# Context keys and values of a decoder's second layer, projected ahead of the first layer's experts and kept in DRAM

## The chip, the cores and the metric

The program runs on one core of a Trainium2 chip. The metric is the device time of one execution in microseconds (us), lower is better. PE is the matrix engine (TensorE), DVE the vector engine, ACT the scalar engine, POOL is GpSimd, SP is the engine that here does nothing but issue DMAs. ACT and POOL issue DMAs too, each on a queue of its own.

## What is computed

A two-layer decoder on x (4 sequences of 512 tokens, width 256) and a context of the same shape. Every step adds its result to x after a layer norm:

```python
x = x + L0_attn(layernorm(x))                 # Mamba block, then attention with 4 heads and a gated FFN
x = x + L0_xattn(layernorm(x), ctx, mask)     # 16 heads of 64, squared relu in place of softmax
x = x + L0_ffn(layernorm(x))                  # 8 experts, each token goes to one
x = x + L1_attn(layernorm(x))                 # block-local causal attention, blocks of 64, 16 heads of 16, rope
x = x + L1_xattn(layernorm(x), ctx, ctx)      # full softmax attention over the context
x = x + L1_ffn(layernorm(x))                  # 16 experts that pick 128 tokens each, and a shared FFN
```

What matters here is `L1_xattn`:

```python
q = (Q @ Wq + bq).reshape(B, L, H, E)
k = (K @ Wk + bk).reshape(B, S, H, E)         # K = V = ctx: neither k nor v depends on x
v = (V @ Wv + bv).reshape(B, S, H, E)
scores = jnp.einsum('blhe,bshe->bhls', q, k)
A = jax.nn.softmax(scale * scores, axis=-1)
out = jnp.einsum('bhls,bshd->blhd', A, v).reshape(B, L, H * E)
return out @ We + be
```

## The kernel before

All engines have a hand-written program each, and wait for one another through semaphores. A `Lane` is a ring of PSUM banks: PE fills a tile (`fill` waits until the tile that was in the bank has been drained), another engine takes it (`take`) and counts `drained` up. SBUF is one array, `arena`, that the stages use one after the other at fixed places, so a buffer of a later stage lies where an earlier one's data were.

The stages, in order of time:

1. Layer 0, per batch (four times): the Mamba block, attention, FFN and cross-attention, 0 to about 1512 us. For the last batch PE, DVE and ACT end with a norm and with the router's logits.
2. Routing (from 1512 us). DVE works out, in some 20 small steps, which slot each token gets (`slot_i`) and which expert each tile of 128 slots belongs to (`te_i`). PE gives it two small matmuls (L962, L963) and then has nothing until tokens have been scattered: POOL scatters 16 chunks to `slots_x` with an indirect DMA each (L2517), ACT waits for all of them and loads the first tile `xg0` (L1633), PE transposes it (L967) and DVE copies it out (`take_slots`, L2127). After the routing steps DVE also zeroes and fills the selection matrices `sel_q` and `sel_k` (six memsets, L2118, and 16 copies, L2123), and sets the ones that stand beside each head's values in `v1o` (L2119).
3. The experts of layer 0: 23 tiles of 128 slots, two buffers (`w1b`, `w2b`, 1 MB each) for the weights, loaded by SP. A tile's weights are asked for as soon as the tile two before it has used the same buffer; PE waits at a tile's start for both matrices of it. PE does W1 (L610, 32 matmul records), the transposes of the next tile (L967) and W2 (L990, 16 records). ACT applies the Gelu and issues the loads of the tokens (`xg0`, 128 KB each, L1639). From tile `W1_AT` = 3 on it also issues, one per tile, the 16 loads of layer 1's weights (`w1_loads`, L1641, 16 to 512 KB each, some 5 MB in all). POOL stores each tile's result to `slots_y` (L2522).
4. POOL gathers the results back (L2526), PE turns the first batch's (`turn_y`, L1033), and layer 1's loop over the batches b = 0..3 begins.
5. One turn of that loop. PE: the rope projections, the values `v2`, then the context keys `yk` (L1089, from `ctxB`, 512 KB that SP loads per batch); then the block scores (L1101), which wait for `qk_here`, 16 small SBUF-to-SBUF DMAs that SP issues one after the other; masks, softmax, transposes (L1112) and weighted sums (L1129) of the four pairs p = 0..3 of blocks follow. Between them lie, for b of 1 and more, the four gate tiles of the shared FFN of the batch before (`ffn_gate(f, m)`, f = b - 1): ACT applies the Gelu (L1665), DVE multiplies (L2178). Then the output projection, a norm, the stacks of the keys (L1168, drained by ACT), the queries `yq` and the context values `yv` (both on the lane that DVE drains). DVE splits the queries into three bf16 parts in five steps (`split_step`, L2215 and L2217), adds the bias to the values (L2264), and PE builds the query stacks (L1168, `w(kq_step, 10)`) and goes on to the cross-attention's scores (L1208).
6. The router and the 16 experts of layer 1, from about 2600 us.

## Time and profile before

| | us |
|---|---|
| median of 3 runs (lowest to highest) | 3049.41 (3048.18 to 3050.52) |
| the profiled execution, its own time | 3046.58 |
| its span in the profile | 3044.8 |
| PE busy | 2701.1 (89%) |
| DVE busy | 1507.2 (50%) |
| ACT busy | 1150.0 (38%) |
| POOL busy | 682.0 (22%) |
| mean granted PE clock, share of 2.4 GHz | 0.936 |

The profile gives for each engine what it did and, before each instruction, how long the engine had been idle and what ended that. PE's fp32 matmuls of 512 columns appear as two records each, so one tile of two such products has four. "PEclk" is the clock that PE was granted: 1.00 is 2.4 GHz and 0.50 is 1.2 GHz. A transfer's "landing" is the time from its issue until its data are there.

### The profile page before, as it was taken

How to read it: one execution, taken by the hardware profiler on the slowest of the kernel's cores; microseconds unless marked ns; L12 is line 12 of the kernel's file. 1: busy time of each engine (PE TensorE's matmuls, PEld its weight loads, DVE VectorE, ACT ScalarE, POOL GpSimd, SP SyncE). 2: the span in 40 equal slices, each digit the busy share in tenths (PEclk: the TensorE clock that was granted, in tenths of full speed). 3: DMA queues.
4: the chain of work that ended last, by engine and by line, in shares of the span. 5: the costliest groups of instructions: out<-in, count | busy, mean ns of one | idle time of the engine just before them, and what ended most of it. 6: DMA issues, size and time to landing. Idle time of an engine off the chain costs nothing. (4 is left out here: it accounts for less than half of the span.)

```text
span 3044.8 us, 40557 instructions
## 1 busy us (share of the span) xinstructions
PE 2701.1 (89%) x16440; PEld 1580.9 (52%) x16481; DVE 1507.2 (50%) x2382; ACT 1150.0 (38%) x1989; POOL 682.0 (22%) x364
## 2 busy tenths in 40 slices
PE   7679999999999999999769888988898988699997
PEld 4265535653285426653368753452543533488776
DVE  5565356733784277635611156446544554644332
ACT  4673245533472255424322235345344343011111
POOL 0254044801571065503320200000000000022222
PEclk9889999999999999999889979999999899799998
DMA  4540003100120003000179610100100101044442
GB/s 191 218 156 22 1 0 115 36 1 1 59 92 1 1 1 129 22 1 0 43 272 335 243 20 7 22 22 1 22 21 1 22 7 73 29 148 158 161 157 64
DMA packets 62130, 218.76 MB, mean 72 GB/s; under 512 B 12293, under 2 KB 28122, under 8 KB 45178
## 3 DMA queue, kind: packets, MB, share of 16 engines
q1 hardware_dynamic: 45802, 187.39, 17.0%
q0 software_dynamic: 9568, 18.75, 2.5%
q10 hardware_dynamic: 6576, 10.05, 0.9%
q8 instruction: 130, 2.13, 0.3%
q14 instruction: 54, 0.44, 0.0%
HBM read 171.98 MB, written 39.99 MB: 70 GB/s over the span
## 5 line engine op out<-in xcount | busy, mean ns | idle before, releaser
L610 PE MATMUL psum<-arena 128*128 128x256 f32 (+7 forms) x4160 | 1081.6, 411 | 67.8 <-ACT arena L1488 11.5
L610 PEld LDWEIGHTS psum<-arena 128*128 128x128 f32 (+1 forms) x4160 | 678.7, 199 | 422.8 <-issue 312.4
L2500 POOL TENSOR_TENSOR arena<-arena 128x1024 f32<-128x1024 f32 x128 | 300.0, 2377 | 111.8 <-DVE arena L1958 96.6
L1958 DVE TENSOR_TENSOR_SCAN arena<-arena,psum 128x512 f32<-128x512 f32 x256 | 291.5, 1201 | 26.5 <-PE psum L751 18.2
L751 PEld LDWEIGHTS psum<-arena 128*128 128x128 f32 x2048 | 243.2, 198 | 47.6 <-ACT arena L1518 40.3
L751 PE MATMUL psum<-arena 128*128 128x128 f32 x2048 | 253.9, 284 | 1.9 <-issue 1.9
L2535 POOL DMA_INDIRECT arena<-xn,arena x32 | 31.6, 988 | 959.0 <-DVE arena L2442 907.2
L2507 POOL TENSOR_TENSOR arena<-arena 128x1024 f32<-128x1024 f32 x32 | 76.0, 2374 | 655.0 <-ACT arena L1606 655.0
L2272 DVE TENSOR_REDUCE arena<-psum 128x1 f32<-128x512 f32 x256 | 162.9, 684 | 84.3 <-PE psum L1208 71.2
L2052 DVE SCALAR_TENSOR_TENSOR arena<-psum,arena 128x1024 f32<-128x1024 f32 x128 | 156.8, 1243 | 80.4 <-PE psum L896 80.1
L1606 ACT ACTIVATE arena<-arena 128x1024 f32<-128x1024 f32 x128 | 146.7, 1146 | 110.0 <-DVE arena L2052 109.9
L1750 ACT ACTIVATE arena<-psum 128x1024 f32<-128x1024 f32 x128 | 129.3, 1024 | 115.6 <-PE psum L1230 115.1
L1790 ACT ACTIVATE arena<-psum 128x256 f32<-128x256 f32 x128 | 49.2, 384 | 320.8 <-PE psum L610 320.8
L1511 ACT ACTIVATE arena<-arena 128x512 f32<-128x512 f32 x256 | 163.0, 708 | 0.0
L2511 POOL TENSOR_TENSOR arena<-arena 128x1024 f32<-128x1024 f32 x64 | 151.2, 2362 | 10.2 <-ACT arena L1606 1.3
L907 PE MATMUL psum<-arena 128*64 128x512 f32 x512 | 138.2, 617 | 15.5 <-ACT arena L1606 7.4
L896 PE MATMUL psum<-arena 64*128 64x512 f32 x512 | 142.5, 638 | 2.7 <-ACT arena L1584 2.7
L2036 DVE RECIPROCAL arena<-arena 128x256 f32<-128x256 f32 x64 | 110.9, 1743 | 46.2 <-ACT arena L1598 46.2
L1405 PE MATMUL psum<-arena 128*128 128x256 f32 x512 | 117.5, 382 | 0.0
L1518 ACT ACTIVATE arena<-arena 128x128 f32<-128x128 f32 x256 | 81.6, 390 | 82.6 <-PE psum L751 60.6
L2465 DVE TENSOR_TENSOR arena<-arena,psum 128x256 f32<-128x256 f32 x128 | 53.2, 421 | 115.7 <-ACT arena L1790 115.2
L1723 ACT ACTIVATE arena<-psum 128x512 bf16<-128x512 f32 x128 | 75.9, 596 | 81.1 <-PE psum L1168 78.5
(298 smaller groups left out, 3210.3 us busy)
## 6 DMA issues: line engine op xcount, KB each, us to landing
arena<-in_W SPq DMA_DIRECT2D x46, 1024.0 KB
arena<-c_rows SPq DMA_DIRECT2D x32, 512.0 KB, 3.8
arena<-in_Wg SPq DMA_DIRECT2D x16, 1024.0 KB, 5.0
arena<-in_Wu SPq DMA_DIRECT2D x16, 1024.0 KB, 7.6
arena<-in_Wd SPq DMA_DIRECT2D x16, 1024.0 KB, 10.0
arena<-in_xT SPq DMA_DIRECT2D x8, 512.0 KB, 5.4
zs_all<-arena SPq DMA_DIRECT2D x4, 1024.0 KB, 3.9
ut_all<-arena SPq DMA_DIRECT2D x4, 1024.0 KB, 8.8
```

Source lines behind the costliest of these rows:

```text
L610: r = mm(dst, w, x, start=i == 0, stop=i == len(pairs) - 1)
L751: r = mm(bank[4 + c][:, q * P:(q + 1) * P], duT[:, q, c * P:(c + 1) * P], diag[n % 2][:, q, :], start=True, stop=True)
L896: i = mm(bank[2 + 2 * (u % SBUFS) + r], xkT[64 * r:64 * r + 64, hp, kc * P:(kc + 1) * P], xqT[64 * r:64 * r + 64, hp, :], start=True, stop ...
L907: i = mm(bank[0][64 * r:64 * r + 64, :], v1[:, kc, 2 * hp + r, :], t2[u % TBUFS][:, r, :], start=kc == 0, stop=kc == NC - 1)
L1511: A_(dA[n % 2][:, c, :], dl[:, c, :], ACT.Exp, scale=aneg[:, c, n:n + 1]).then_inc(dA_ready.sem, 1)
L1606: A_(t2[u % TBUFS], rl[u % RBUFS], ACT.Square, scale=0.125, bias=vec[:, V_NB:V_NB + 1])\
L1750: A_(pr1[v % 4], psum[:, 4 + 2 * (v % 2):6 + 2 * (v % 2), :], ACT.Exp).then_inc(p1_ready.sem, 1)
L1958: V.tensor_tensor_scan(hs[n % 3][:, c, :], dA[n % 2][:, c, :], bank[4 + c], 0.0, ALU.mult, ALU.add)\
L2052: V.scalar_tensor_tensor(rl[u % RBUFS], t, minus_nb8, bound[:, kc, :].unsqueeze(1).broadcast_to([P, 2, L]), ALU.max, ALU.min).then_inc(rel ...
L2272: V.reduce_max(negm1[:, qc, h:h + 1], t, AX.X, negate=True).then_inc(s1_max.sem, 1)
L2500: nc.gpsimd.tensor_tensor(h, h, c_all[:, n % CBUFS, :].unsqueeze(1).broadcast_to([P, 2, L]), ALU.mult)\
L2511: nc.gpsimd.tensor_tensor(t, t, t2[kc], ALU.add).then_inc(tsum_step.sem, 1)
```

## The change

- The keys (with bias `bk`) and the values (with bias `bv` and the ones) of all four batches are projected right behind PE's two routing matmuls, for which the four contexts are loaded into the place of `y_all` (the views `xnf`). Lane `LCK` (banks 2 and 3) is drained by ACT into `kf_st`, lane `LCV` (banks 4 to 7) by DVE into `v1o_st`. The order on PE is 4 value tiles, 8 key tiles, 4 value tiles.
- PE waits until both lanes are drained before it goes on to the transposes of the first expert tile. DVE's drains stand behind its routing steps and ahead of its work on `sel_q` and `sel_k`.
- ACT stores `kf_st` (512 KB) and `v1o_st` (1 MB) of batch b to DRAM scratch at expert tile `KV_AT` + b, b = 0..3, with `KV_AT` = 3. `w1_loads` move from ACT, beside the expert tiles, to SP, in the last batch of layer 0 behind the drains of `xq`, with the loads of the four contexts ahead of them.
- In layer 1's loop `yk` and `yv` are gone, with their drains on ACT and DVE (the removed lines of those two engines are not shown), and SP loads `kf` and `v1o` of a batch from the scratch: for batch 0 once the experts' last store has landed, later ones once the buffers are free.
- `ffn_gate(f, 0)`, with its Gelu and its product, moves from behind `block_scores(0)` to ahead of it.

```diff
+        kf_all, v1o_all = dram("kf_all", (B, P, KD * L)), dram("v1o_all", (B, P, NC * LH * 2 * LE))
...
+                if b == B - 1:
+                    sp.wait_ge(LA.drained.sem, LA.drained.at(LA.upto("xq", 8), b))
+                    for i in range(B):
+                        sp.dma_start(xnf[i], batch("ctxT", i)).then_inc(ld_cB.sem, 16)
+                    for dst, src in w1_loads:
+                        sp.dma_start(dst, A[src]).then_inc(ld_w1.sem, 16)
...
-            def load_ctx(b):
-                sp.dma_start(ctxB, A["ctxT"][b:b + 1].rearrange("a p k n -> p (a k) n")).then_inc(ld_cB.sem, 16)
+            def load_kv(b):
+                if b >= 1:
+                    sp.wait_ge(kq_step.sem, kq_step.at(5, b - 1))
+                sp.dma_start(kf.rearrange("p a b -> p (a b)"), kf_all[b]).then_inc(ld_kf.sem, 16)
+                if b >= 1:
+                    sp.wait_ge(LBO.full.sem, LBO.full.at(4, b - 1))
+                sp.dma_start(v1o.rearrange("p c h e -> p (c h e)"), v1o_all[b]).then_inc(ld_v1o.sem, 16)
...
             load_x(0)
+            sp.wait_ge(st_kv.sem, st_kv.at(16 * 2 * B))
             load_x(1)
-            sp.wait_ge(scattered.sem, 16 * CH)
-            load_ctx(0)
+            for j in range(2):
+                sp.wait_ge(st_y[j].sem, st_y[j].at(0, (NT0 + 1 - j) // 2))
+            load_kv(0)
...
+            pe.wait_ge(ld_w1.sem, 16 * len(w1_loads))
+            pe.wait_ge(ld_cB.sem, 16 * B)
+            def value_tile(n):
+                t = LCV.fill(pe, 0, "v", n)
+                for c in range(2):
+                    o = (2 * (n % 2) + c) * P
+                    r = acc(t[:, c * D:(c + 1) * D], [(xnf[n // 2][:, k, o:o + P], w_yv[:, k, :]) for k in range(KD)])
+                r.then_inc(LCV.full.sem, 1)
+            for n in range(4):
+                value_tile(n)
+            for n in range(KD * B):
+                acc(LCK.fill(pe, 0, "k", n), [(w_yk[:, k, n % KD * P:(n % KD + 1) * P], xnf[n // KD][:, k, :])
+                                             for k in range(KD)]).then_inc(LCK.full.sem, 1)
+            for n in range(4, 2 * B):
+                value_tile(n)
+            pe.wait_ge(LCK.drained.sem, LCK.drained.at(KD * B))
+            pe.wait_ge(LCV.drained.sem, LCV.drained.at(2 * B))
...
-                pe.wait_ge(ld_cB.sem, ld_cB.at(16, b))
-                for m in range(KD):
-                    project(LBA, f"yk{b}", m, w_yk, ctxB)
+                if f >= 0:
+                    dve_has(f"rope_b{b}", 6)
+                    ffn_gate(f, 0)
...
                 block_scores(0)
-                if f >= 0:
-                    ffn_gate(f, 0)
                 block_scores(1)
...
-                for i in range(2):
-                    t = LBV.fill(pe, 0, f"yv{b}", i)
-                    for c in range(2):
-                        r = acc(t[:, c * D:(c + 1) * D],
-                                [(ctxB[:, k, (2 * i + c) * P:(2 * i + c + 1) * P], w_yv[:, k, :]) for k in range(KD)])
-                    r.then_inc(LBV.full.sem, 1)
                 key_stacks(4)
...
-                for dst, src in w1_loads[n - W1_AT:n - W1_AT + 1] if n >= W1_AT else ():
-                    act.dma_start(dst, A[src]).then_inc(ld_w1.sem, 16)
+                if 0 <= n - KV_AT < B:
+                    b = n - KV_AT
+                    act.wait_ge(LCK.drained.sem, LCK.drained.at(KD * (b + 1)))
+                    act.dma_start(kf_all[b], kf_st[b].rearrange("p a b -> p (a b)")).then_inc(st_kv.sem, 16)
+                    act.wait_ge(LCV.drained.sem, LCV.drained.at(2 * (b + 1)))
+                    act.dma_start(v1o_all[b], v1o_st[b]).then_inc(st_kv.sem, 16)
...
+            dve.wait_ge(ld_w1.sem, 16 * len(w1_loads))
...
+            for b in range(B):
+                r = V.memset(heads[b][:, :, :, LE:2 * LE], 1.0)
+            link(m_step, r)
+            for n in range(2 * B):
+                t, i = LCV.take(dve, 0, "v", n), n % 2
+                V.tensor_tensor(heads[n // 2][:, 2 * i:2 * i + 2, :, 0:LE],
+                                b_yv.rearrange("p (h e) -> p h e", h=LH).unsqueeze(1).broadcast_to([P, 2, LH, LE]),
+                                t.rearrange("p (c h e) -> p c h e", c=2, h=LH), ALU.add).then_inc(LCV.drained.sem, 1)
```

How the order changes, at the three places that the prediction speaks of. First DVE, from the last routing step to the first copy of an expert tile. Before (L2118 and L2123 make `sel_q` and `sel_k`, L2127 is `take_slots`, L2138 copies a tile's result):

```order
L2113 TENSOR_SCALAR arena<-arena 128x23 [waits m_step]
L2118 MEMSET arena 128x512 x6
L2119 MEMSET arena 128x64x16
L2120 MEMSET arena 128x256
L2123 COPY arena<-arena 128x8x16 [waits m_step]
L2123 COPY arena<-arena 128x8x16 x15
L2127 COPY arena<-psum 128x256 [waits g_full] x2
```

With the change (L2154 sets ones, L2158 drains the value tiles, then `sel_q`, `sel_k` and `take_slots`):

```order
L2149 TENSOR_SCALAR arena<-arena 128x23 [waits m_step]
L2154 MEMSET arena 128x64x16 [waits ld_w1]
L2154 MEMSET arena 128x64x16 x3
L2158 TENSOR_TENSOR arena<-arena,psum 128x32x16 [waits a_norm,m_step]
L2158 TENSOR_TENSOR arena<-arena,psum 128x32x16 [waits a_norm] x7
L2164 MEMSET arena 128x512 x6
L2168 COPY arena<-arena 128x8x16 [waits m_step]
L2168 COPY arena<-arena 128x8x16 x15
L2172 COPY arena<-psum 128x256 [waits g_full] x2
```

Eight drains, each of which waits for PE (`a_norm` is lane `LCV`), now stand ahead of the memsets and copies, and all of them ahead of the first `take_slots`.

Second PE, in layer 1's loop, from the queries to the first query stack (L1168, in the change L1201, are stacks; L610, in the change L626, projections; `kq_step` is DVE's split). Before:

```order
L610 MATMUL psum<-arena 128x512 [waits dve_drained]
L610 MATMUL psum<-arena 128x512
L610 MATMUL psum<-arena 128x256 [waits dve_drained]
L610 MATMUL psum<-arena 128x256 x3
L610 MATMUL psum<-arena 128x256 [waits dve_drained]
L610 MATMUL psum<-arena 128x256 x3
L1168 MATMUL psum<-arena 128x512 [waits act_drained]
L1168 MATMUL psum<-arena 128x512 x2
L1168 MATMUL psum<-arena 128x512 [waits act_drained]
L1168 MATMUL psum<-arena 128x512 x2
L1168 MATMUL psum<-arena 128x512 [waits act_drained,kq_step]
```

With the change:

```order
L626 MATMUL psum<-arena 128x512 [waits dve_drained]
L626 MATMUL psum<-arena 128x512
L1201 MATMUL psum<-arena 128x512 [waits act_drained]
L1201 MATMUL psum<-arena 128x512 x2
L1201 MATMUL psum<-arena 128x512 [waits act_drained]
L1201 MATMUL psum<-arena 128x512 x2
L1201 MATMUL psum<-arena 128x512 [waits act_drained,kq_step]
```

The two value tiles (the rows of 256 columns) are gone; the wait for the split stays behind the last two key stacks.

Third PE in batch 1, from the last tile of `v2` to the first weight transposes (L1101, in the change L1136, are block scores, L1112, in the change L1147, the transposes). Before:

```order
L610 MATMUL psum<-arena 128x512 [waits act_drained,ld_cB]
L610 MATMUL psum<-arena 128x512
L610 MATMUL psum<-arena 128x512 [waits act_drained]
L610 MATMUL psum<-arena 128x512
L1101 MATMUL psum<-arena 64x64 [waits act_drained,qk_here]
L1101 MATMUL psum<-arena 64x64 x31
L610 MATMUL psum<-arena 128x512 x4
L1101 MATMUL psum<-arena 64x64 [waits mask_done]
L1101 MATMUL psum<-arena 64x64 x31
L1112 MATMUL psum<-arena 128x128 [waits act_drained,bp_ready]
```

With the change:

```order
L626 MATMUL psum<-arena 128x512 [waits dve_drained]
L626 MATMUL psum<-arena 128x512 x3
L1136 MATMUL psum<-arena 64x64 [waits act_drained,qk_here]
L1136 MATMUL psum<-arena 64x64 x31
L1136 MATMUL psum<-arena 64x64 [waits mask_done]
L1136 MATMUL psum<-arena 64x64 x31
L1147 MATMUL psum<-arena 128x128 [waits act_drained,bp_ready]
```

The keys are gone, gate tile 0 stands where they stood, and between the two groups of block scores PE has nothing.

## Rows read from the trace of the kernel before

**Rows 1.** The page, part 1: busy time, share of the span, instructions.

```profile
PE 2701.1 (89%) x16440; PEld 1580.9 (52%) x16481; DVE 1507.2 (50%) x2382; ACT 1150.0 (38%) x1989; POOL 682.0 (22%) x364
```

**Rows 2.** Timeline, 1490 to 1560 us: start, duration, engine, line, operation, [idle before <-releaser].

```profile
1520.01 3.19 DVE L2118 MEMSET arena<- 128x512 uint32 x6
...
1524.59 1.80 DVE L2123 COPY arena<-arena 128x128 bf16<-128x128 bf16 x16
...
1545.43 0.69 PE L967 MATMUL psum<-arena 128*128 128x128 f32 x2 [30.45 <-DMA arena<-slots_x]
...
1546.16 0.43 DVE L2127 COPY arena<-psum 128x256 f32<-128x256 f32 x1 [19.77 <-PE psum L967]
...
1546.73 5.98 PE L610 MATMUL psum<-arena 128*128 128x128 f32 x32 [0.61 <-DVE arena L2127]
```

**Rows 3.** Windows: busy us (count) per engine, PEclk, DMA share, GB/s; one 50 us stretch.

```profile
1500.00:1550.00 50.00, 14.69 (x67) 13.61 (x67) 13.99 (x50) 2.74 (x4) 15.67 (x16) 0.50 0.52 184
```

**Rows 4.** Timeline of PE, two expert tiles in a row.

```profile
1556.64 3.73 PE L610 MATMUL psum<-arena 128*128 128x128 f32 x32
...
1564.30 3.73 PE L610 MATMUL psum<-arena 128*128 128x128 f32 x32
```

**Rows 5.** Waits of PE, 1500 to 1750 us: total us, times, longest us.

```profile
PE psum L610 <- DMA arena<-b_parts: 2.7, 3, 1.5
```

**Rows 6.** Windows of one expert tile's length each, columns as in rows 3.

```profile
1592.69:1600.35 7.66, 7.66 (x53) 6.93 (x52) 0.85 (x2) 2.29 (x9) 0.54 (x1) 1.00 0.77 263
...
1600.35:1608.01 7.66, 7.66 (x52) 6.75 (x51) 0.85 (x2) 2.16 (x9) 0.54 (x1) 1.00 0.98 385
```

**Rows 7.** DMA issues, 1545 to 1740 us: count, KB each, median us to landing.

```profile
arena<-slots_x ACTq DMA_DIRECT2D x22, 128.0 KB, 6.1
```

**Rows 8.** Timeline, 1715 to 1890 us: last expert store, first gather, first turned tile.

```profile
1732.99 1.00 POOL L2526 DMA_INDIRECT arena<-slots_y,arena  x1 [2.25 <-DMA slots_y<-arena]
...
1739.72 1.94 PE L1033 MATMUL psum<-arena 128*128 128x128 f32 x8 [10.29 <-DMA arena<-slots_y,arena]
```

**Rows 9.** Timeline, 2036 to 2066 us: batch 1 around the context values.

```profile
2039.91 7.17 PE L610 MATMUL psum<-arena 128*128 128x512 f32 x24
...
2044.44 0.70 DVE L2215 CAST arena<-arena 128x1024 bf16<-128x1024 f32 x1
...
2046.92 1.46 PE L1168 MATMUL psum<-arena 128*128 128x512 bf16 x6
...
2048.42 0.69 DVE L2215 CAST arena<-arena 128x1024 bf16<-128x1024 f32 x1
...
2049.03 1.28 DVE L2264 TENSOR_TENSOR arena<-arena,psum 128x512 f32<-128x512 f32 x2
...
2049.40 2.76 PE L1168 MATMUL psum<-arena 128*128 128x512 bf16 x11 [1.02 <-DVE arena L2215]
```

**Rows 10.** Windows, 14 us that follow, columns as in rows 3.

```profile
2050.00:2064.00 14.00, 13.74 (x60) 5.23 (x59) 10.24 (x18) 8.93 (x15) 0.00 (x0) 1.00 0.00 1
```

**Rows 11.** Timeline, 1950 to 2062 us: batch 1's block attention on PE.

```profile
1972.37 0.91 PE L1101 MATMUL psum<-arena 16*64 16x64 f32 x64
...
1978.20 1.09 PE L1112 MATMUL psum<-arena 128*128 128x128 f32 x8 [0.44 <-ACT arena L1702]
...
1979.13 3.65 PE L610 MATMUL psum<-arena 128*128 128x512 f32 x8
...
1982.72 1.44 PE L1129 MATMUL psum<-arena 64*64 64x16 f32 x64
...
1989.71 6.23 PE L610 MATMUL psum<-arena 128*128 128x512 f32 x8
```

**Rows 12.** Windows, 7 us of it, columns as in rows 3.

```profile
1988.00:1995.00 7.00, 5.77 (x9) 2.68 (x10) 4.06 (x7) 3.28 (x4) 0.00 (x0) 0.51 0.00 0
```

**Rows 13.** Timeline of PE, 2174 to 2240 us: the same gate tile of batch 2.

```profile
2197.24 4.88 PE L610 MATMUL psum<-arena 128*128 128x512 f32 x8
```

**Rows 14.** Timeline, 1715 to 1890 us: batch 0's first weight transposes.

```profile
1785.48 1.97 PE L1112 MATMUL psum<-arena 128*128 128x128 f32 x8 [2.69 <-ACT arena L1702]
```

More of the change, by code:

```diff
@@ L256, in decoder_program @@
         h0T, y0 = [take(KH, P) for _ in range(2)], [take(D) for _ in range(2)]
+        kf_st, v1o_st = [take(KD, L) for _ in range(B)], [take(NC * LH * 2 * LE) for _ in range(B)]
         top[0] = after_w1
-        ctxB = take(KD, L)
         blocks_at = top[0]
@@ L586, in _ @@
                 if b + 1 < B:
[L587 to L588 removed]
+                    load_kv(b + 1)
                 sp.wait_ge(LBA.drained.sem, LBA.drained.at(LBA.upto(f"xn{b}", 2)))
@@ L991, in _ @@
                 r.then_inc(ym_full.sem, 1)
-            pe.wait_ge(ld_w1.sem, 16 * len(w1_loads))
             pe.wait_ge(sel_made.sem, 1)
@@ L1628, in _ @@
             round_end(act, rd_a, 0)
+            act.wait_ge(ld_cB.sem, 16 * B)
+            for n in range(KD * B):
+                t = LCK.take(act, 0, "k", n)
+                A_(kf_st[n // KD][:, n % KD, :], t, ACT.Identity, bias=vec[:, V_BK + n % KD:V_BK + n % KD + 1])\
+                    .then_inc(LCK.drained.sem, 1)
             act.wait_ge(scattered.sem, 16 * CH)
@@ L1672, in drain_out @@
                     .then_inc(LFA.drained.sem, 1)
+            act.wait_ge(st_kv.sem, st_kv.at(16 * 2 * B))
             norm_squares(0, xc0, sq0)
@@ L1687, in _ @@
                     r.then_inc(LBA.drained.sem, 1)
-                for m in range(KD):
-                    t = LBA.take(act, 0, f"yk{b}", m)
-                    A_(kf[:, m, :], t, ACT.Identity, bias=vec[:, V_BK + m:V_BK + m + 1]).then_inc(LBA.drained.sem, 1)
+                if f >= 0:
+                    ffn_gelu(f, 0)
                 def drain_pair(p):
@@ L2178, in ffn_mult @@
                 V.tensor_tensor(gu1[:, m, :], sg1[m % 2], bank[FFN_AT[m] + 1], ALU.mult).then_inc(LFV.drained.sem, 1)
+            dve.wait_ge(st_kv.sem, st_kv.at(16 * 2 * B))
+            link(m_step, V.memset(nm_parts, 0.0))
             add_y(0)
@@ L2242, in _ @@
                         .then_inc(b_step.sem, 1)
-                    if f >= 0 and p == 0:
-                        ffn_mult(f, 0)
                     w(b_step, 3 * p + 3)
@@ L2261, in _ @@
                     split_step(5, qf, q_parts, i)
-                for i in range(2):
-                    t = LBV.take(dve, 0, f"yv{b}", i)
-                    V.tensor_tensor(v1o[:, 2 * i:2 * i + 2, :, 0:LE],
-                                    b_yv.rearrange("p (h e) -> p h e", h=LH).unsqueeze(1).broadcast_to([P, 2, LH, LE]),
-                                    t.rearrange("p (c h e) -> p c h e", c=2, h=LH), ALU.add).then_inc(LBV.drained.sem, 1)
                 def row_max(u):
```

29 lines of the change are left out of this document (16 added, 13 removed).

## The prediction

> **What bounds the kernel now.** I read the page's first part, then the timeline of each place that the change touches, then windows for the clock and the DMA rate. PE is busy for 89% of the span [rows 1], so at first sight every PE microsecond that is taken out of layer 1's loop is a gain. Whether it is one is decided place by place: by what PE would wait for if the work were not there. Four places count.
>
> The first is the routing. PE has nothing for 30.45 us, from 1514.98 us on, until the scattered tokens are back; then transposes, DVE's copy `take_slots`, and the first expert tile at 1546.73 [rows 2]. PE's granted clock is 0.50 there, the level of 1.2 GHz [rows 3]. DVE's selection matrices take 3.19 and 1.80 us behind the routing steps, and DVE then idles 19.77 us before `take_slots` [rows 2]: today they cost nothing.
>
> The second is the experts. A tile takes 7.66 us on PE [rows 4], which runs without a gap except for 2.7 us of waits for weights in the whole stage [rows 5]. The DMA engines are not far behind: their share is 0.77 in one tile and 0.98, at 385 GB/s, in another [rows 6].
>
> The third is the context values in the loop. PE runs queries and values as one block of 24 records, 2039.91 to 2046.92; the key stacks follow, and then PE waits 1.02 us, until 2049.40, for DVE's split of the queries, whose last step starts at 2048.42 and takes 0.69 us. DVE adds the value bias only behind that [rows 9]. So what ends that stretch is DVE's split, not PE. Behind it PE sets the pace: 13.74 of the next 14 us are busy, DVE 10.24 and ACT 8.93 [rows 10].
>
> The fourth is the block attention. In batch 1 the first block scores start at 1972.37, the transposes of the weights, which wait for ACT's exponential, at 1978.20, then come gate tile 1 and, with no idle time, the weighted sums at 1982.72 [rows 11]. What ends the wait for the block scores is `qk_here`, 16 DMAs that SP issues one by one; the keys end just when they land.
>
> **The change, part by part.** *Projections in the gap.* One batch's keys and values have the shapes of one batch's queries and values, 7.01 us from start to start (2039.91 to 2046.92, rows at full clock) [rows 9]; four batches are 28.0 us. PE starts them at half clock. The first expert tile shows what such a start costs: 5.98 us against 3.73, 2.3 us [rows 2, 4]. So PE ends at 1514.98 + 28.0 + 2.3 = 1545.3. DVE drains the last value tile in 0.64 us [rows 9], with some 0.2 us to be told of it: 1546.1. Only then come the selection matrices, 3.19 + 1.80 = 5.0, with 0.2 for their wait in between: 1551.3. `take_slots` follows (0.43), and the first expert tile starts 0.57 us behind its start, as today (1546.16 to 1546.73) [rows 2]: about 1551.8 in place of 1546.73, **+5.1 us**. PE idles about 5 us more before it, so it starts cold again. Ends: +2.7 (the projections at full clock from the start) and +6.5 (a longer cold start, or a lane that stalls). ACT's eight key drains and DVE's memsets of ones lie beside PE; the scatter on POOL ends before 1545.43 and is no longer last.
>
> *Loads and stores beside the experts.* The 5 MB of layer 1's weights and the contexts are now loaded in the last cross-attention, where PE does not wait for DMAs and the queues are all but idle: 0, and SP's 20 issues stand ahead of waits that come much later. With them the 2.7 us of waits should go. In their place four stores of 0.5 and 1.05 MB, 1.57 MB per tile, stand at tiles 3 to 6. A tile's own traffic is 2 x 1.05 MB of weights and 2 x 0.13 MB of tokens and results, 2.36 MB, 6.1 us at the 385 GB/s of [rows 6]; the store adds 4.1, together 10.2 against 7.66: 2.55 us late per tile, 10.2 in four. One tile's spare 1.5 us of being ahead is to be subtracted once, and the 2.7: **+6.0 us**. Ends: -2.7 (the stores yield to the loads) and +9.8 (nothing ahead, and one cold start of 2.3). The Trainium skill ("DMA: Bandwidth & Descriptors", section "Where 436 GB/s comes from") says that the memory side holds one core to about 358 GB/s between HBM and SBUF; by it this part would be some 3 us dearer, an estimate from that page. The trace disagrees, with 385 GB/s over a whole tile, and the measurement decides.
>
> *First load of keys and values.* It starts when the last expert store has landed, which is when POOL starts to gather, at 1732.99; PE waits for the first four gathers until 1739.72 [rows 8]. 1.57 MB need 4.1 us of the same engines. Nearest row: 128 KB of tokens beside the weights took 6.1 us to land [rows 7], while the fourth gather now has about 3 us from its start to PE's. Ends 0 and +3.2; the loads are over before the fourth gather would be, so I take the middle, **+1.5 us**. Later loads stand behind `og` and ahead of the store of `xn1`, with microseconds to spare: 0. DVE's and ACT's waits for `st_kv` are met long before: 0.
>
> *Values out of the loop.* Without them PE goes from the queries straight to the last key stacks and is through with them at about 2044.7. DVE's split begins when the queries are there and is not shortened; PE waits until 2049.40 as before, 4.7 us in place of 1.02. Gain: 0. DVE's 1.28 us lay in its own wait: 0. But the clock: before, this stretch is busy enough that PE stays at full clock. In the trace PE lost it over less, in batch 1 around 1988 [rows 12], and gate tiles then take 6.23 us or 4.88 in place of 3.65 [rows 11, 13]. So PE comes back at half clock, and PE is what the next 14 us wait for. Prices of a cold start: 2.3 (above), 2.6, 1.2; I take 2.1, **+8.4 us** for four batches; ends 0 and 4 x 2.6 = 10.4. The Trainium skill ("TensorE: Matmul & The Clock Gate", section "HAM oscillation — how this bites in real kernels") describes just this: short work and then a wait, again and again, so that each return is at half rate. It speaks against this change, and the trace agrees, with 0.51 over seven microseconds that PE comes back to.
>
> *Keys out of the loop, gate tile 0 ahead.* The tile (3.65 us) takes the place of the keys (the same number of records) ahead of `qk_here`: 0 gained at the block scores. Its old place stays empty: from the first block scores to the transposes, 1972.4 to 1978.2, PE has only a second group of block scores. In batch 0, where nothing stands there today either, the transposes take 1.97 us in place of 1.09 [rows 11, 14]: half clock. So gate tile 1 of batches 1 to 3 runs cold, and the weighted sums, which start when it ends, are late. Ends: 0 and 2.6 + 0.9; the later tiles are cold today too, and DVE has one product less at this point, so I take 1.8, **+5.4 us** for three. In batch 0 nothing covers `qk_here` now; the work behind waits for DVE: **+0.3**, ends 0 and 2.6.
>
> The sum is 5.1 + 6.0 + 1.5 + 8.4 + 5.4 + 0.3 = **+26.7 us**. The profiled execution took 3046.6 us, 2.8 below the median of the runs; on the median, 3049.4 + 26.7 = **3076 us**.
>
> **The rivals.** *The clock holds.* If PE stays at full clock through the emptier stretches, the last three terms go: 5.1 + 6.0 + 1.5 = 12.6, **3062 us**. For it: the clock now survives the 1.02 us wait. Against it: batch 0's transposes, which show half clock behind the same empty stretch.
>
> *The stores hide.* If the DMA engines serve the weights first, or mix stores and loads at well over 385 GB/s, the expert stage has no waits at all: 26.7 - 6.0 - 2.7 = 18.0, **3067 us**. For it: stores and loads have opposite directions. Against it: the share of 0.98 with an additional load (`w1_loads`) of only 0.26 MB in that tile. With both, +3.9, **3053 us**, no change.
>
> *PE's work was the bound: faster.* 28.0 us of PE work leave the loop for a gap of 30.45 us. If PE, not DVE, ended the stretch before the query stacks, each batch would lose its 7.01 us: -28.0 + 12.6 = -15.4, **3034 us**. That decides at one point: whether PE without the values reaches the wait for the split later than 2049.1. For it: PE's 89%. Against it: PE waits there already with the values in place, and would arrive 4.4 us early.
>
> That the change does not do what it says has next to no chance: the orders of PE and DVE show each step where the description puts it.
>
> **How the numbers follow.** My forecast, all terms near their sizes, has 0.64, with a range of its own of 3064 to 3089. The clock holds: 0.13. The stores hide: 0.12. Both, no change: 0.05. Faster: 0.05. 0.01 is left for dearer than all bounds. The range reaches from below the clock's case, 3058, to 3090, and leaves out the last three and the edges. A measurement of this kernel tells about 0.2%, 6.1 us, from no change: faster 0.05, same 0.05, slower 0.90.
>
> **What would show it.** Right: the first expert tile starts near 1552, behind DVE's selection matrices, not behind a DMA; PE waits 2 to 3 us for weights in each of tiles 3 to 7, and hardly later; PE waits about 4.7 us for the split in each batch, the first query stacks take longer, and the granted clock is 0.50 there; batches 1 to 3 show transposes of 1.97 us for pair 0. Wrong: a turn of the loop that is shorter than today's by several microseconds, full clock at the query stacks, or tiles 3 to 6 at 7.66 us.

## The result, and the profile of the changed kernel

The changed kernel takes **3072.14 us**, the median of 5 runs (3058.43 to 3076.10), against 3049.41 for the kernel before on the same chip (5 runs, 3046.75 to 3053.95). The ratio is 1.0066, 95% interval 1.0048 to 1.0083: slower by 0.5 to 0.8%. The forecast was 3076 in 3058 to 3090, with 0.90 on slower. The profiled execution has a span of 3070.3 us where the kernel before has 3044.8, 25.5 more; the sum of the prediction was 26.7. The medians differ by 22.7 us, and the five runs of the change spread over 18 us, so the ratio and its interval are the better measure of the size.

I cut both traces at the same instructions. All times are in us; "put at" is what the prediction had for the stretch. In the rows for four batches the stretches are added up:

| stretch | before | after | differs | put at |
|---|---|---|---|---|
| routing matmul to first expert tile | 32.12 | 40.10 | +8.0 | +5.1 |
| first expert tile to first gather | 186.26 | 193.00 | +6.7 | +6.0 |
| first gather to first turned tile | 6.73 | 6.84 | +0.1 | +1.5 |
| turned tile to first block scores, batch 0 | 39.93 | 41.35 | +1.4 | +0.3 |
| the same, batches 1 to 3 | 132.60 | 130.27 | -2.3 | 0 |
| first block scores to first key stack, four batches | 195.13 | 199.05 | +3.9 | +5.4 |
| first key stack to first query stack | 98.68 | 98.64 | 0 | 0 |
| first query stack to first score | 10.37 | 17.94 | +7.6 | +8.4 |
| first score to next batch's turned tile | 250.60 | 255.05 | +4.5 | 0 |
| last first score to the end | 577.77 | 573.38 | -4.4 | 0 |

They add to 25.5. The stretches that the forecast priced come to 27.7 (8.0 + 6.7 + 0.1 + 1.4 + 3.9 + 7.6); those that it put at nothing are not small, and cancel but for -2.2. Each kernel has one profiled execution, and stretches of unchanged code differ between them: the one from the turned tile to the first block scores of batch 0 takes 39.93, 43.74 and 44.80 us in the three profiled kernels that keep keys and values in the loop. So the +1.4 of that row is no evidence of anything, and a few us in any single row are weak evidence. The rows, view by view.

**The gap.** The timeline of the changed kernel, 1500 to 1575 us, columns as in [rows 2]:

```profile
1514.84 30.64 PE L626 MATMUL psum<-arena 128*128 128x256 f32 x96
...
1545.52 0.69 DVE L2158 TENSOR_TENSOR arena<-arena,psum 128x512 f32<-128x512 f32 x1 [1.04 <-PE psum L626]
1546.27 3.19 DVE L2164 MEMSET arena<- 128x512 uint32 x6
...
1546.43 0.37 SPq L560 DMA_DIRECT2D arena<-in_W  x1
...
1549.49 1.73 DVE L2168 COPY arena<-arena 128x128 bf16<-128x128 bf16 x16
...
1551.13 0.42 DVE L2172 COPY arena<-psum 128x256 f32<-128x256 f32 x1
```

The projections end at 1545.5, as worked out, and the selection matrices and `take_slots` stand where the prediction put them: DVE would let PE go at about 1551.7. But SP issues the first expert's weights only at 1546.43. In the kernel before that row stands at 1521.21:

```profile
1521.21 0.37 SPq L550 DMA_DIRECT2D arena<-in_W  x1
```

PE's first credit for that buffer (the signal that it is free to be loaded), `pe.sem_inc(hm_full.sem, hm_full.ahead)`, stands behind the projections in the new code, and SP waits for it. So PE waits for a DMA. PE's timeline of the changed kernel, 1546 to 1640 us, the answer to [rows 4]:

```profile
1554.78 5.42 PE L626 MATMUL psum<-arena 128*128 128x128 f32 x32 [8.05 <-DMA arena<-b_parts]
...
1564.13 3.73 PE L626 MATMUL psum<-arena 128*128 128x128 f32 x32
...
1579.45 3.73 PE L626 MATMUL psum<-arena 128*128 128x128 f32 x32
...
1590.40 3.84 PE L626 MATMUL psum<-arena 128*128 128x128 f32 x32 [3.13 <-DMA arena<-b_parts]
...
1599.62 3.84 PE L626 MATMUL psum<-arena 128*128 128x128 f32 x32 [1.28 <-DMA arena<-b_parts]
...
1609.04 3.84 PE L626 MATMUL psum<-arena 128*128 128x128 f32 x32 [1.49 <-DMA arena<-b_parts]
...
1619.21 5.47 PE L626 MATMUL psum<-arena 128*128 128x128 f32 x32 [2.24 <-DMA arena<-b_parts]
...
1628.61 3.73 PE L626 MATMUL psum<-arena 128*128 128x128 f32 x32
```

**The stores.** In place of 7.66 us the tiles stand 10.95, 9.22, 9.42 and 10.17 us apart from the first tile with a store (1579.45) on. PE comes out of the last wait at the lower clock (a cold start), which makes it 9.40 to the next tile: 10.9 us late in all. PE's waits of the stage, 1500 to 1770 us, answer to [rows 5] (2.7 us then); 8.0 of them are the first tile's:

```profile
PE psum L626 <- DMA arena<-b_parts: 16.2, 5, 8.0
```

**The loop.** PE's timeline of batch 1, 1975 to 2085 us, answers to [rows 9, 11] (L1201 are stacks, L1235 the first scores):

```profile
1992.56 0.91 PE L1136 MATMUL psum<-arena 16*64 16x64 f32 x64 [1.44 <-DMA arena<-arena]
...
1998.40 1.97 PE L1147 MATMUL psum<-arena 128*128 128x128 f32 x8 [2.46 <-ACT arena L1740]
2000.16 4.45 PE L626 MATMUL psum<-arena 128*128 128x512 f32 x8
2004.54 1.44 PE L1164 MATMUL psum<-arena 64*64 64x16 f32 x64
...
2069.95 4.45 PE L1201 MATMUL psum<-arena 128*128 128x512 bf16 x12 [4.26 <-DVE arena L2262]
2074.24 1.03 PE L1235 MATMUL psum<-arena 128*128 128x512 bf16 x4
```

The transposes of pair 0 take 1.97 us in place of 1.09, gate tile 1 4.45 in place of 3.65. PE waits 4.26 us for the queries' split in place of 1.02, and the query stacks that follow are cold: from the first stack to the first score it is 5.07 us in batch 0, at a granted clock of 0.50, and 4.29 in the others, in place of 2.59. From the first key stack to the first query stack all four batches take 24.65 to 24.67 us in both kernels: the values that left this stretch, 3.5 us of PE's work per batch, gave nothing.

**The clock, further on.** What I had not seen is what follows the stacks. Windows of batch 0's cross-attention in the kernel before, columns as in [rows 3]:

```profile
1878.95:1887.15 8.20, 7.51 (x40) 1.95 (x42) 4.37 (x8) 4.10 (x5) 0.00 (x0) 1.00 0.00 0
1895.35:1903.65 8.30, 6.61 (x38) 1.64 (x37) 5.75 (x9) 4.40 (x5) 0.00 (x0) 1.00 0.00 0
```

and of the changed kernel at the same places behind its first score:

```profile
1898.10:1906.30 8.20, 7.66 (x34) 1.51 (x34) 4.17 (x7) 3.67 (x4) 0.00 (x0) 0.79 0.00 0
1914.50:1922.80 8.30, 6.76 (x34) 1.55 (x31) 4.44 (x8) 2.94 (x4) 0.00 (x0) 0.83 0.00 1
```

The code is the same there, with the same waits of 1.54 us for DVE, and twice PE comes out of one at the lower level (2.4 GHz is the full one, 1.2 the lower), so that it gets through 34 records where it was 40 and 38. The last 573 us are the same code in both kernels too. Where their 4.4 us come from no row tells: the other kernels below, the two without the change among them, have 574 to 580 there, so the changed kernel's 573.4 is the shortest of a spread rather than a gain.

### The profile page after: what moved, and what is told of

It reads as the page before. It is cut to its first block and busy times, and to the rows that moved or that the text cites. A ratio compares the mean times of both kernels' runs of the same rounds, so it can differ in the third digit from the quotient of the medians.

```text
span 3070.3 us, 40624 instructions
## 1 busy us (share of the span) xinstructions
PE 2724.7 (89%) x16481; PEld 1589.7 (52%) x16481; DVE 1511.5 (49%) x2385; ACT 1153.5 (38%) x1992; POOL 681.9 (22%) x364
## 5 line engine op out<-in xcount | busy, mean ns | idle before, releaser
L626 PE MATMUL psum<-arena 128*128 128x256 f32 (+7 forms) x4160 | 1087.9, 414 | 75.7 <-DMA arena<-b_parts 16.2
L626 PEld LDWEIGHTS psum<-arena 128*128 128x128 f32 (+1 forms) x4160 | 684.7, 201 | 431.9 <-issue 312.1
L1201 PE MATMUL psum<-arena 128*128 128x512 bf16 x384 | 101.9, 403 | 22.9 <-DVE arena L2262 17.0
L2506 DVE TENSOR_TENSOR arena<-arena,psum 128x256 f32<-128x256 f32 x128 | 53.4, 421 | 115.7 <-ACT arena L1826 115.1
```

The lines of the kernel that those rows point to most:

```text
L626: r = mm(dst, w, x, start=i == 0, stop=i == len(pairs) - 1)
```

## The experiments

Theory T, after the result: five causes in different places add up (late first weights, stores beside loads, transposes behind an emptier stretch, query stacks behind a longer wait, and the lower clock in the cross-attention behind them). Rivals stand with each run. The kernel before ran beside them each time: median 3048.91 (14 runs) for the first four, 3051.57 (25) for the next four, 3052.32 (20) for the last four. The ratios are to these.

### The first weights: the credit ahead of the projections

```diff
+            pe.sem_inc(hm_full.sem, hm_full.ahead)
             pe.wait_ge(ld_w1.sem, 16 * len(w1_loads))
...
-            pe.sem_inc(hm_full.sem, hm_full.ahead)
             pe.wait_ge(ld_g.sem, 16)
```

> The changed kernel, with PE's credit for the first expert weights (sem_inc of hm_full) ahead of the projections in place of behind them. Theory: in the changed kernel the first expert tile starts at 1554.8 us because SP may ask for the first weights only at 1546.4; with the credit back at 1515 it starts when DVE is through with the selection matrices, at 1551.8 (3.0 us earlier), and the time is about 3 us shorter than the changed kernel's 3072. Rival (the weights are late for another reason, for instance because the DMA engines are busy with the scatter): still 1554.8.

Measured: 3065.55 us (3060.51 to 3067.53, 4 runs), ratio 1.0054 (1.0036 to 1.0072). The timeline at its first expert tile, up to 1552 us, where the window ends:

```profile
1549.51 0.42 DVE L2172 COPY arena<-psum 128x256 f32<-128x256 f32 x1
...
1550.07 2.26 PE L626 MATMUL psum<-arena 128*128 128x128 f32 x9 [4.97 <-DVE arena L2172]
```

The tile now waits for DVE and starts 37.10 us behind the routing matmul, 3.00 earlier than in the changed kernel. So the late credit cost 3.0 us there, and the prediction's path was the next one in line, at +5.0 for +5.1. From the first expert tile to the first gather it is another 2.1 us shorter (190.93 for 193.00), since the stores come to cost less too.

### The selection matrices ahead of the value drains

The 22 instructions that make them (L2164, L2168) move ahead of DVE's loop of value drains, with the credit moved too.

> As the run before, and DVE makes the selection matrices ahead of the drains of the value tiles. Theory: nothing then stands between the last drain (1546.2) and take_slots, so that the first expert tile starts near 1547.3, 7.5 us earlier than in the changed kernel, and takes 3.7 to 4.5 us in place of 5.4, since PE has hardly been idle. In all about 8 to 9 us less than the changed kernel. Rival (the wait for the tokens or the weights ends last anyway): 1551 or later.

Measured: 3056.99 us (3054.73 to 3063.11, 6 runs), ratio 1.0031 (1.0018 to 1.0044).

The timeline up to 1549 us:

```profile
1547.08 0.42 DVE L2172 COPY arena<-psum 128x256 f32<-128x256 f32 x1 [0.55 <-PE psum L1004]
...
1547.65 1.58 PE L626 MATMUL psum<-arena 128*128 128x128 f32 x12 [0.61 <-DVE arena L2172]
```

The tile starts 32.73 us behind the routing matmul, 0.6 later than in the kernel before, and warm: its 32 records take 3.81 us. The 28 us of projections fit the gap; what cost time was the order of instructions on PE and on DVE. It saves 7.4 us there of the changed kernel's 8.0.

### The stores in smaller pieces

Each 1.05 MB store is cut in two, and the twelve pieces of 0.5 MB are issued one per tile, at tiles 3 to 14.

> The changed kernel, with its 6.3 MB of stores in twelve pieces of 0.5 MB at the expert tiles 3 to 14, in place of four pairs of 1.57 MB at tiles 3 to 6. Theory (DMA rate): a piece adds 1.36 us to a tile's 6.1 us of transfers, which fits in 7.66, so the waits of PE for weights in tiles 3 to 7 (8.1 us, and a cold start of 1.7) shrink to at most 3 us in all; 6 to 9 us less than the changed kernel. Rival (stores disturb the loads whatever their rate): waits of some 8 us stay, spread over more tiles.

Measured: 3066.45 us (3060.63 to 3068.12, 4 runs), ratio 1.0056 (1.0038 to 1.0073); from the first expert tile to the first turned one 200.75 us, against 199.84. No gain in the stage: this expectation failed. (The median is 5.7 us below that of the changed kernel, but the intervals overlap, and the profiled execution is shorter only in batch 1 of the loop, where 49.92 and 82.00 us stand for 52.73 and 85.07.) PE's waits of the stage:

```profile
PE psum L626 <- DMA arena<-b_parts: 11.6, 6, 8.0
...
PE psum L1003 <- DMA arena<-slots_x: 5.7, 6, 1.6
```

Without the first tile's 8.0 the waits for weights fell from 8.2 to 3.6 us, but waits for tokens came in their place. The token loads stand behind the stores on ACT's queue, and their median time to landing rose; that the shared queue is the reason was not tried apart:

```profile
v1o_all<-arena ACTq DMA_DIRECT2D x8, 512.0 KB, 8.7
...
arena<-slots_x ACTq DMA_DIRECT2D x21, 128.0 KB, 7.3
```

In the changed kernel the latter is 5.6.

### The wait for the split, covered

Eight products of 256 columns with no reader are computed behind the queries, where the values stood: 3.5 us of work more in each batch.

```diff
                     project(LBV, f"yq{b}", m, w_yq, xn)
+                for i in range(2):
+                    for c in range(2):
+                        acc(bank[6][:, c * D:(c + 1) * D], [(xn[:, k, (2 * i + c) * P:(2 * i + c + 1) * P], w_yv[:, k, :]) for k in range(KD)])
```

> The changed kernel, with eight products of the shape of the value tiles behind the queries in each turn of the loop; their result is written to a free PSUM bank and used by nobody, so it is extra work for PE of 3.5 us per batch. Theory (clock): PE stays at full clock, waits about 1 us for the split as before the change, and the way from the first query stack to the first score is 2.59 us again in place of 5.07, 4.29, 4.29 and 4.29; some 7.6 us less in these stretches although 14 us of work are added, and the first query stack starts at the same distance (24.66 us) from the first key stack. Rival (PE was the bound, or the slower stacks have another cause): the distance grows by 2 to 3.5 us per batch, or the stacks stay slow.

Measured: 3058.55 us (3051.57 to 3065.11, 9 runs), ratio 1.0033 (1.0019 to 1.0047), whose interval lies just below that of the changed kernel. With 14 us more work for PE the kernel is faster: by 13.6 us in the medians and in the profiled executions, by 10 in the ratios. Batch 1:

```profile
2059.98 2.76 PE L1201 MATMUL psum<-arena 128*128 128x512 bf16 x11 [1.01 <-DVE arena L2265]
2062.58 1.02 PE L1238 MATMUL psum<-arena 128*128 128x512 bf16 x4
```

Key stacks to query stacks take 24.67 us as ever, the query stacks 2.59 to 2.60 in place of 5.07 and 4.29, and the bodies (first score to the next batch's turned tile, three batches) 249.0 in place of 255.05. These two give 7.5 + 6.1 = 13.6 us, also the difference of the spans; the rest cancels. So the 7.6 us of the table belong to that wait. For the 4.5 of the body that is not shown. The body takes 82.0 to 86.9 us in the kernels here, and cold stacks do not decide it: with the stores in pieces, batch 1's stacks were cold (4.10 us), and its body took 82.00 where batches 0 and 2 took 84.90 and 85.07; in the two last kernels below all stacks are warm, and bodies take 86.85 once in one, 85.06 and 86.32 in the other.

### Gate tile 0 back behind the first block scores

The values and keys stay out of the loop; the gate tile, ACT's gelu and DVE's product go back to their old places.

> The changed kernel, with gate tile 0 (its two projections, Gelu and product) back behind the first block scores, where the kernel before had it; the keys stay out of the loop, so that nothing stands in the wait for qk_here. Theory (the empty place behind the block scores costs a cold start of gate tile 1): batches 1 to 3 go from the first block scores to the first key stack in about 52 us again in place of 52.74, 53.23 and 53.43, but PE comes cold to the block scores, which costs some of it; 0 to 3 us less than the changed kernel in all. Rival (gate tile 0 ahead is the better place, since it fills a wait of 5 us): the stretch grows by up to 3.65 us per batch, because the tile now lies on the path in it; 3 to 10 us more.

Measured: 3079.08 us (3077.85 to 3080.67, 4 runs), ratio 1.0081 (1.0062 to 1.0099). The median lies 7 us above that of the changed kernel, but the intervals overlap, so the stretches have to tell it. Batch 1:

```profile
1993.85 1.29 PE L1133 MATMUL psum<-arena 16*64 16x64 f32 x64 [4.86 <-DMA arena<-arena]
1995.07 5.92 PE L626 MATMUL psum<-arena 128*128 128x512 f32 x8
```

The rival came true. The transposes are warm again, but the wait for `qk_here` is now bare, the block scores come out of it cold, and the gate tile takes 5.92 us. From block scores to key stacks batches 1 to 3 take 54.4 us each, where the change has 52.7 to 53.4 and the kernel before 51.7 to 52.4. That is 3.5 us more than the changed kernel in four batches; the query stacks take 1.5 more, and the bodies 3.9 less. Once the keys are gone, one 3.65 us tile has two holes to cover; ahead is the better one, by little. So the cost of this term comes from the keys' absence, not from the gate tile's place.

### Layer 1's weights early, in the kernel before

The loads of `w1_loads` move from ACT's turns of the expert tiles to SP in the last batch of layer 0; nothing else.

> The kernel before, with one part of the change alone: SP loads the weights of layer 1 in the last batch of layer 0, and ACT no longer beside the expert tiles. Theory: PE's waits for weights (2.7 us) and tokens (0.3) in the expert stage go, nothing else moves: 2 to 3 us less than the kernel before, from the first expert tile to the first turned tile 190.0 us in place of 192.99. Rival (these waits have another cause): 192.99 and no change.

Measured: 3047.78 us (3041.07 to 3055.05, 10 runs), ratio 0.9985 (0.9970 to 0.9999). The experts' stretch takes 189.03 us in place of 192.99, and PE's waits for weights in it are 0.2 us. This part of the change is worth 4.0 us by itself, of which the prediction counted 2.7, the waits of [rows 5]. The rest is in the distances from tile to tile: behind the first one they exceed 7.66 us by 4.3 us in all in the kernel before, and by 0.4 here. Besides the waits for weights there was one of 0.3 for tokens, and the records next to a wait ran slower (3.84 us for 3.73, for example).

### The split in two halves, with and without the change

DVE splits each half of the queries when that half is there, in ten smaller steps in place of five, and PE waits for the second half only before its first stack of it.

```diff
-                w0(LBV.drained, LBV.upto(f"yq{b}", 2))
-                for i in range(5):
-                    split_step(5, qf, q_parts, i)
+                    w0(LBV.drained, LBV.upto(f"yq{b}", m + 1))
+                    for i in range(5):
+                        split_step(5 + 5 * m, qf[:, m, :], [x[:, m, :] for x in q_parts], i)
```

On the changed kernel:

> The changed kernel, with DVE's split of the queries done for the two halves of the channels one after the other (ten steps of 512 columns in place of five of 1024); the first eight query stacks need the first half alone. Theory (DVE's split ends that stretch): the first query stack starts when the first half is split, about 4 us earlier (20.7 us behind the first key stack in place of 24.66), PE idles under 1 us there and keeps full clock, so that the stacks take 2.6 us again: about 4 + 1.7 us per batch, some 20 us less than the changed kernel, near 3052. Rival (the second half, or DVE's extra work per step, comes too late): the gain is under 2 us per batch.

and on the kernel before:

> The kernel before, with the same split in halves. Theory: PE has the values to do until 2046.9 and then the key stacks until 2048.2, and waits 1.0 us for the split; so the halves can give 1 us per batch at most, 2 to 4 us in all, and the values' work is now on the path. Rival (the split was never what ended the stretch): nothing.

Measured: on the change 3049.75 us (3043.77 to 3057.57, 10 runs), ratio 0.9992 (0.9980 to 1.0005); on the kernel before 3053.94 (3050.40 to 3057.16, 10 runs), ratio 1.0005 (0.9993 to 1.0016). The same edit takes some 22 us off one kernel and nothing off the other; the 2 to 4 us expected of the latter did not come. From key stacks to the next turned tile, batches 0 to 2: 109.25, 110.80 and 112.35 us before, 114.62, 114.03 and 114.04 with the change; with the halves 111.20 to 111.30 and 107.12 to 107.26. Batch 1 of the change with halves, where the stacks start warm after 0.67 us:

```profile
2055.09 2.98 PE L1201 MATMUL psum<-arena 128*128 128x512 bf16 x12 [0.67 <-ACT arena L1761]
```

With DVE's wait out of the way the removed values, 3.5 us of PE's work, are worth 4 us per batch. That settles what ended the stretch before. A part of the 4 us is the edit's own cost in the kernel before: there DVE drains the second half of the queries only behind the split of the first, and PE waits 0.9 us for that in each batch looked at (0 to 2), in the middle of the values.

### The stores early, and what they cost at all

On the kernel with the credit and the matrices moved, ACT issues each key store right behind its batch's key drains, in the wait for the scatter, and the value stores as eight halves at tiles 0 (four), 1 (two), 2 and 3:

> The kernel with the earlier credit and the selection matrices ahead (a2_credit_sel), with the stores moved into the time in which the DMA engines have room: each batch's keys (0.5 MB) are stored as soon as they are drained, in the wait for the scatter, and the values in halves of 0.5 MB, four at expert tile 0, two at tile 1, one each at tiles 2 and 3. Theory (total DMA time, and the tokens' loads that queue behind stores on ACT's queue): the room before tile 2 takes most of the 6.3 MB, so from the first expert tile to the first turned tile it is 191 to 194 us in place of 198.65, some 5 to 7 us less than a2_credit_sel. Rival (stores cost the same wherever they stand): 198 again, or the first tile is late because the scatter or the first weights are.

Beside it a kernel without the stores, whose layer 1 cross-attention reads other data of the same size:

> The kernel a2_credit_sel without its eight stores of keys and values; so that nothing reads what was never written, the loop loads the context in place of the keys and 1 MB of an expert's weights in place of the values (same sizes, same times, wrong numbers: layer 1's cross-attention is not computed). Theory: the stores are all that the expert stage lost, so first expert tile to first turned tile is 189 to 190 us, against 198.65 with them and 192.99 in the kernel before. Rival (the changed stage has another loss, for instance the load of keys and values beside the gathers): 192 or more.

Measured: the early stores 3057.81 us (3051.37 to 3068.74, 10 runs), ratio 1.0020 (1.0005 to 1.0036); without stores 3049.85 (1 run). From the first expert tile to the first turned one: 190.93 us and 189.77, where the kernel with late stores has 198.65. The stores therefore cost 8.9 us there, and 1.2 when early; add 1.4 to both, since the kernel without stores started its first tile cold (5.22 us for 3.81). But the first tile came 38.27 us behind the routing matmul, not 32.7. The timeline of the early stores shows why:

```profile
1533.62 0.69 ACT L1664 ACTIVATE arena<-psum,arena 128x512 f32<-128x512 f32 x1 [1.60 <-PE psum L626]
...
1539.31 0.69 ACT L1664 ACTIVATE arena<-psum,arena 128x512 f32<-128x512 f32 x1 [5.00 <-issue]
...
1540.05 10.60 PE L626 MATMUL psum<-arena 128*128 128x512 f32 x36 [3.59 <-issue]
```

ACT, which drains the keys, was held for 5.00 us by nothing that the profile shows, behind its second store issue and before the third (1532.05 and 1540.03). PE stopped for 3.59 us until ACT's next drain was over; the keys have two banks, so it had none free. What held ACT was not tried apart. SP's queue has no drains behind it and may be the better place for these issues, which was not tried either. The gain of 7.7 us was given back but for 2.2.

### Together

The early stores with the halves of the split, and the same with two tiles of products without a reader (3.65 us) behind the first block scores in batches 1 to 3:

> c1_early with the split in halves. Theory: the parts add up: the 22 us of the halves, the 15 us that the earlier credit and the selection matrices gave, and the 5 to 7 of the stores, 3072 - 42 = 3030 to 3040, against 3049 to 3052 for the kernel before; faster than both. Rival (parts overlap, or the clock takes back what one gives): 3040 to 3050.

> c3_best with the key projections' shapes (two tiles, 3.65 us) run behind the first block scores of batches 1 to 3, their result used by nobody. Theory (the empty place there costs a cold start): transposes of pair 0 take 1.09 us in place of 1.97, and the way from the first block scores to the first key stack is 51.8 to 52.4 us in batches 2 and 3 in place of 53.1 to 53.4; 1 to 4 us less than c3_best, although 11 us of work are added. Rival: the work costs its own time on PE's path, up to 3.65 us per batch.

Measured: **3040.73 us** (3034.09 to 3043.65, 8 runs), ratio 0.9960 (0.9945 to 0.9976), and **3038.27** (3034.42 to 3043.09, 7 runs), ratio 0.9953 (0.9934 to 0.9973). Both are faster than both kernels, by 0.4 to 0.5% against the kernel before. The expected 3030 to 3040 was missed by 0.7: the first tile stands 34.52 us behind the routing matmul where 32.7 was reckoned with. ACT is late again, but it shows in another place: PE stops only 0.78 us in the projections, and then waits for the first tokens, whose load ACT issues behind its last key store (1543.18, the load at 1543.83):

```profile
1547.35 0.41 PE L1004 MATMUL psum<-arena 128*128 128x128 f32 x2 [1.62 <-DMA arena<-slots_x]
```

The two tiles without a reader do what they should at their place. Batch 1 without it, and with it:

```profile
1980.57 1.97 PE L1147 MATMUL psum<-arena 128*128 128x128 f32 x8 [2.35 <-ACT arena L1744]
1982.33 4.37 PE L626 MATMUL psum<-arena 128*128 128x512 f32 x8
```

```profile
1980.81 1.09 PE L1147 MATMUL psum<-arena 128*128 128x128 f32 x8 [0.44 <-ACT arena L1747]
1981.74 3.65 PE L626 MATMUL psum<-arena 128*128 128x512 f32 x8
```

In all, block scores to key stacks takes 152.95 us in batches 1 to 3 in place of 156.33; the two totals can't be told apart.

## Why the prediction was right, and where it was not

**What bounds each place: right in three of four.** The reading of [rows 9], that DVE's split and not PE ends the stretch before the query stacks, is what gave the sign. 24.67 us before and after show it, and the halves show it from the other side. *Query stacks*, put at +8.4 (2.1 per batch): +7.6, and the cover takes 7.5 away. PE's wait was 4.26 us for 4.7. "The clock holds" is out: batch 0's stacks ran at a granted clock of 0.50, as forecast, and the twelve records take 5.23 and 4.45 us where the eleven recorded before took 2.76.

**Projections in the gap: +5.1 put, +8.0 measured.** The step that failed is "`take_slots` follows (0.43), and the first expert tile starts 0.57 us behind its start". The path through DVE was right to 0.1 us, as the moved credit shows; it was not the last. The sum had no term for what PE signals late when 28 us of work are put ahead of its other instructions, though in the changed kernel's text the credit stands behind them. I had named "behind DVE's selection matrices, not behind a DMA" as a sign of being right; a DMA is what came.

**Loads and stores beside the experts: +6.0 put, +6.7 measured.** The mechanism was right, its parts were off both ways. Three of the four tiles with a store took 9.2 to 10.2 us for 10.2; the DMA engines moved 419, 407 and 401 GB/s in them (windows from 1590.40, 1599.62 and 1609.04 on) where 385 was reckoned with. PE was not a tile ahead at the first store (3.13 us at once, put at 1.0), and the last wait ended cold, 1.74 us, which I had only in the upper end. So the stores cost 10.9 for the 8.7 put. Against that, layer 1's weights gave 4.3 in place of 2.7; one wait for tokens, with what ran slower behind it (+0.7), and a shorter first tile (-0.6) make up the rest. The Trainium skill ("DMA: Bandwidth & Descriptors", section "Where 436 GB/s comes from") has about 358 GB/s for the memory side; the DMA view of 1550 to 1760 us, in slices of 5.25 us, disagrees further than [rows 6] did (the program runs on one core):

```profile
GB/s 412 259 228 250 328 343 423 401 423 419 403 383 413 345 176 275 262 346 320 232 349 311 280 379 216 323 378 225 336 340 317 218 343 379 204 348 1 108 329 110
```

**First load of keys and values: +1.5 put, +0.1 measured.** The load and the gathers did not hinder each other; the middle between the ends was a guess, and the lower end was right.

**Keys out, gate tile 0 ahead: +5.4 put, +3.6 measured** in batches 1 to 3, and +0.4 in batch 0 for 0.3. The transposes were 0.88 us late, as read from [rows 14]; gate tile 1 took 4.45, 4.88 and 5.08 us for 3.65, because the clock was back before it ended (in batch 1 0.54 from 2000.1 to 2002.0, 1.00 from there to 2004.5). The three stretches grew by only 0.4, 1.5 and 1.7 us, so the step that was too dear is that the whole delay reaches the end of the stretch. In batch 0 PE now waits 4.88 us for `qk_here`, and from the start of the rope projections to the block scores it takes 0.3 us more (25.28 for 24.98), as put; the other 1.1 of that row's +1.4 lies ahead of them, where both kernels do the same.

**Put at nothing: the cross-attention behind the stacks, +4.5.** The step that failed is to price the cold start by the instructions that it slows alone, with nothing for what follows. PE's clock fell twice more in batch 0's cross-attention where before it had not. The cover has the 4.5 away again, but bodies of 82.0 to 86.9 us, long ones behind warm stacks too, leave the cause open. Against it stand -2.3 and -4.4 of unchanged code in other places, which I can only name. With these, an error of the sum of 1.2 us is luck: terms missed by +2.9, +0.7, -1.4, -1.8, -0.8, +4.5, +1.5 (batch 0) and -6.7.

**The rivals.** "The stores hide" is out by the waits. "PE's work was the bound: faster" was wrong of this change. With the halves PE's work does count, 4 us per batch, and that brings the changed kernel level with the one before (0.9992, 0.9980 to 1.0005), not to 3034.

## What to carry to other kernels

Work taken out of a loop is worth what the next waiter lets it be worth: before moving it, look for the wait that ends the stretch, and shorten that with the same edit (here some 22 us between the change with and without it). Work put into an idle gap of an engine goes ahead of everything that the engine signals, so list its credits (what other engines wait for from it) and the drains behind it, not only the data that it waits for. And a wait that a moved piece covered may be worth covering again, with work that nobody reads if need be, when what comes behind it is on the path.

## What the runs showed of the hardware

- More work made the kernel faster: 3.5 us of products per batch took 10 (by the ratios) to 13.6 us (by the medians) off the time. The Trainium skill ("TensorE: Matmul & The Clock Gate", section "HAM oscillation — how this bites in real kernels") describes the returns at half rate; the trace agrees (5.07 and 4.29 us from the first query stack to the first score, against 2.59).
- Stores and loads together moved 401 to 423 GB/s in five slices in a row, 26 us. That mixing them gives more is not shown: the first slice of the same view has 412 with weight loads and no store.
- The same code of the cross-attention took 82.0 to 86.9 us per batch in these kernels, with warm and with cold starts; what decides it is open.
- Loads of 128 KB on a queue with twelve stores of 0.5 MB between them took 7.3 us to land (median), in place of 5.6 with eight stores in four tiles.
- ACT, which had issued a second 0.5 MB store during the scatter, stood still for 5.00 us; why is open.
